# Fetching one column of gathered rows in two of three chunks with plain DMAs from SyncE

## The reference

```python
def _mean_aggregate(x, edge_index, num_nodes):
    src, dst = (edge_index[0], edge_index[1])
    msgs = x[src]
    summed = jax.ops.segment_sum(msgs, dst, num_segments=num_nodes)
    ...
    return summed / jnp.maximum(counts, 1.0)[:, None]
agg = _mean_aggregate(x, edge_index, x.shape[0])
out = agg @ W_l.T + b_l + x @ W_r.T
out = relu(out) + x
```

## Time and profile before

| | us |
|---|---|
| median of three runs | 4668.51 |
| profiled execution, its own time | 4669.47 |
| its span | 4667.1 |
| first gather of layer 1 begins | 2469.35 |
| last gather of layer 1 begins | 4469.16 |
| last store of layer 1's sums issued | 4483.83 |

### The profile page before, as it was taken

One profiled execution on the slowest core, in us unless ns is written; L12 is line 12 of the kernel. 1 busy time (PEld: TensorE's weight loads), 2 busy tenths in 40 slices (PEclk: granted clock), 3 DMA queues, 4 the chain that ended last, 5 costly groups with the idle time before them and its releaser, 6 DMA issues. The chain is left out here.

```text
span 4667.1 us, 26336 instructions
## 1 busy us (share of the span) xinstructions
PE 922.2 (20%) x3111; PEld 611.6 (13%) x3111; DVE 2264.2 (49%) x9482; ACT 397.2 (9%) x994; POOL 3394.4 (73%) x3539
## 2 busy tenths in 40 slices
PE   6301101111120000000292222112222222101036
PEld 6301001011010000000141111001111111100025
DVE  2107665665566656655563434434334334334347
ACT  2001001001010000000051000000000000000015
POOL 6677777777777777777556777777777777777764
PEclk6556555555555555555595555555555555555569
DMA  9813333333333222222285666665666666666669
GB/s 339 307 38 117 119 92 94 119 103 102 100 103 111 77 78 88 87 77 78 89 280 179 209 233 219 210 230 205 215 226 221 218 221 226 218 215 214 208 213 320
DMA packets 347657, 793.59 MB, mean 170 GB/s; under 512 B 78438, under 2 KB 217035, under 8 KB 323972
## 3 DMA queue, kind: packets, MB, share of 16 engines
q1 hardware_dynamic: 150162, 378.14, 23.0%
q0 software_dynamic: 139424, 279.69, 19.8%
q10 hardware_dynamic: 57938, 134.62, 7.6%
HBM read 420.40 MB, written 371.83 MB: 170 GB/s over the span
## 5 line engine op out<-in xcount | busy, mean ns | idle before, releaser
L460 POOL DMA_INDIRECT sb_big<-x,sb_idx x1564 | 1524.3, 975 | 513.1 <-issue 476.5
L460 POOL DMA_INDIRECT sb_big<-zu_rows,sb_idx x1564 | 1479.6, 946 | 490.9 <-issue 476.6
L1264 DVE SCALAR_TENSOR_TENSOR sb_big<-sb_big,sb_keepc 128x256 f32<-128x256 f32 x1518 | 741.8, 489 | 534.6 <-DMA sb_big<-x,sb_idx 481.9
L642 PE MATMUL ps_T<-sb_ident,sb_xg 128*128 128x128 f32 x308 | 87.3, 380 | 2513.7 <-DMA sb_xg<-x 1407.7
L1034 DVE TENSOR_TENSOR sb_big<-ps_V,sb_big 128x2176 f32<-128x2176 f32 x46 | 111.5, 2425 | 596.7 <-DMA sb_big<-zu_rows,sb_idx 596.7
L642 PEld LDWEIGHTS ps_T<-sb_ident,sb_xg 128*128 128x128 f32 x308 | 55.0, 195 | 2558.2 <-issue 1932.0
L1028 DVE TENSOR_TENSOR_SCAN ps_V<-ps_V,sb_big 128x34 f32<-128x34 f32 x2944 | 357.1, 211 | 14.8 <-issue 14.8
L1264 DVE SCALAR_TENSOR_TENSOR sb_big<-sb_scratch,sb_keepc,sb_big 128x256 f32<-128x256 f32 x46 | 22.3, 485 | 697.9 <-DMA sb_big<-x,sb_idx 660.9
L1077 DVE TENSOR_TENSOR_SCAN sb_big<-ps_E,sb_big 128x34 f32<-128x34 f32 x2944 | 355.4, 205 | 1.6
L460 POOL DMA_INDIRECT sb_hn<-rows,sb_nidx x196 | 190.4, 971 | 89.2 <-issue 56.7
L776 ACT COPY sb_tileT<-ps_T 128x256 f32<-128x256 f32 x154 | 56.9, 369 | 1419.1 <-PE ps_T L642 1416.8
(11 more groups left out here) (233 smaller groups left out, 1946.4 us busy)
## 6 DMA issues: line engine op xcount, KB each, us to landing
rows<-sb_big SPq DMA_DIRECT2D x46, 2816.0 KB, 10.1
rows<-sb_big SPq DMA_DIRECT2D x46, 1536.0 KB, 6.0
rows<-sb_big ACTq DMA_DIRECT2D x46, 1224.0 KB, 4.6
z_at_start<-sb_zero ACTq DMA_DIRECT2D x46, 1088.0 KB, 9.5
sb_big<-z_at_start SPq DMA_DIRECT2D x46, 1088.0 KB, 5.0
sb_xg<-in_x_dram SPq DMA_DIRECT2D x42, 768.0 KB, 6.0
own<-sb_hn SPq DMA_DIRECT2D x28, 896.0 KB, 8.9
sb_big<-own SPq DMA_DIRECT2D x28, 896.0 KB, 5.2
```

The source lines that it names most:

```text
L460: pool.indirect_dma_start(to, None, table, bass.IndirectOffsetOnAxis(ap=index.bitcast(U32), axis=0), **more).then_inc(done, 16)
L642: mm = pe.transpose(T[b % depth][:, k * P:(k + 1) * P], xg[0][:, b, k * P:(k + 1) * P], ident[:, :])
L1264: dve.scalar_tensor_tensor(out=slot1[s][:, j, :], in0=before, scalar=keepc[:, j:j + 1], in1=slot1[s][:, j, :], op0=ALU.mult, op1=ALU.add). ...
```

## The change

The last column (33) of a chunk in buffer 0 or 1 is no longer gathered by GpSimd, except in chunk 0. SyncE fetches it: for every partition one plain DMA of one row of 1 KB from `x1` into `slot1[s]`, at a row number that SyncE has in a register. The row numbers come out of `src_i`, first by a DMA of 128 words into a staging row on one partition, then in eight loads of 16 registers. The fetch is in two halves of 64 rows, which stand in SyncE's list behind the first and behind the second store of the chunk two before. VectorE waits for it ahead of column 33 alone. SyncE's last looped round is written out.

```diff
+            rows_at = [sp.alloc_register(f"row{k}") for k in range(RB)]
+            def stage_rows(i, s):
+                    sp.dma_start(stage[0:1, s, :], src_i[:, bass.ds((S1 * i + s) * C + C - 1, 1)]
+                                 ).then_inc(stage_loaded[s], 16)
+            def fetch_rows(i, s, half):
+                if half == 0:
+                    sp.wait_ge(stage_loaded[s], 16 * (i + s))
+                    sp.sem_inc(gate, 1)
+                    wait(sp, r_stored[s], 32 * i)
+                    sp.sem_inc(gate, 1)
+                for p0 in range(half * P // 2, (half + 1) * P // 2, RB):
+                    sp.load(rows_at, stage[0:1, s, p0:p0 + RB])
+                    for k in range(RB):
+                        row = sp.snap(rows_at[k], min_val=0, max_val=N - 1)
+                        sp.dma_start(slot1[s][p0 + k:p0 + k + 1, C - 1, :], x1[bass.ds(row, 1), :]
+                                     ).then_inc(r_fetched[s], 16)
             def store_rows1(i, s):
                 c = S1 * i + s
+                ahead = (i, 2) if s == 0 else (i + 1, s - 1)
+                if by_sync(*ahead):
+                    stage_rows(*ahead)
                 sp.wait_ge(col_summed, c * C + CA)
                 sp.dma_start(edge_cols(rows1, c)[:, 0:CA, :], ...)
+                if by_sync(*ahead):
+                    fetch_rows(*ahead, 0)
                 sp.wait_ge(car1_saved, c + 2)
                 sp.dma_start(edge_cols(rows1, c)[:, CA:C, :], ...)
+                if by_sync(*ahead):
+                    fetch_rows(*ahead, 1)
...
-                for j in range(C):
+                for j in range(C - 1 if by_sync(i, s) else C):
                     gather(slot1[s][:, j, :], x1, idx[s][:, j:j + 1], r_gathered[int(j >= CA)][s])
...
                     elif j == CA:
-                        dve.wait_ge(r_gathered[1][s], 16 * (C - CA) * (i + 1))
+                        rest = C - CA
+                        by_gpsimd = rest + (rest - 1) * i if s == 0 else (rest - (s == 1)) * (i + 1)
+                        dve.wait_ge(r_gathered[1][s], 16 * by_gpsimd)
+                    if j == C - 1 and by_sync(i, s):
+                        dve.wait_ge(r_fetched[s], 16 * P * (i + s))
```

More of the change, by code:

```diff
@@ L75, in gnn_kernel @@
     LOOK = S1 * C
+    RB = 16
     NZ = 4
@@ L191, in gnn_kernel @@
         idx = [sb(f"idx{s}", [P, C], I32) for s in range(S1)]
+        stage = sb("stage", [1, 2, P], I32)
         nidx = [sb(f"nidx{s}", [P, GB], I32) for s in range(2)]
@@ L267, in gnn_kernel @@
         r_stored = sems("r_stored", S1); car1_saved = sem("car1_saved")
+        stage_loaded = sems("stage_loaded", 2); r_fetched = sems("r_fetched", 2)
         DA = 15
@@ L275, in gnn_kernel, with by_sync @@
         block = ctx.enter_context(nc.Block())
+        def by_sync(i, s):
+            first = isinstance(i, int) and i == 0
+            beyond = isinstance(i, int) and S1 * i + s >= NCH
+            return s < 2 and not (first and s == 0) and not beyond
         def edge_cols(dram, c):
@@ L410, in _ @@
                 sp.wait_ge(n_stored[0][s], 32 * (NG // 2))
+            rows_at = [sp.alloc_register(f"row{k}") for k in range(RB)]
+            def stage_rows(i, s):
+                with nc.allow_non_contiguous_dma(reason="a word of each partition"):
+                    sp.dma_start(stage[0:1, s, :], src_i[:, bass.ds((S1 * i + s) * C + C - 1, 1)]
[12 more added lines that the diff above has]
+                                     ).then_inc(r_fetched[s], 16)
             def store_rows1(i, s):
                 c = S1 * i + s
+                ahead = (i, 2) if s == 0 else (i + 1, s - 1)
+                if by_sync(*ahead):
+                    stage_rows(*ahead)
                 sp.wait_ge(col_summed, c * C + CA)
                 sp.dma_start(edge_cols(rows1, c)[:, 0:CA, :], slot1[s][:, 0:CA, :]).then_inc(r_stored[s], 16)
+                if by_sync(*ahead):
+                    fetch_rows(*ahead, 0)
                 sp.wait_ge(car1_saved, c + 2)
                 sp.dma_start(edge_cols(rows1, c)[:, CA:C, :], slot1[s][:, CA:C, :]).then_inc(r_stored[s], 16)
+                if by_sync(*ahead):
+                    fetch_rows(*ahead, 1)
             bg_load(1, 0)
+            stage_rows(0, 1)
+            for half in range(2):
+                fetch_rows(0, 1, half)
             for s in range(S1):
                 store_rows1(0, s)
-            with sp.Fori(1, NG) as i:
+            with sp.Fori(1, NG - 1) as i:
                 bg_store(1, i - 1)
@@ L429, in _ @@
                     store_rows1(i, s)
+            bg_store(1, NG - 2)
+            bg_load(1, NG - 1)
+            for s in range(S1):
+                store_rows1(NG - 1, s)
             bg_store(1, NG - 1)
```

## The result

The changed kernel took 5226.19 us (median of four runs, 5207.68 to 5249.59) against 4660.88 us before on the same chip: a ratio of 1.1202, 95% interval 1.1151 to 1.1253. The 4660.88 us are the median of four runs, the three of before and one more, so the kernel lost 565.3 us. The forecast was 5217 us, 548.5 more than 4668.5. The profiled execution took 5238.41 us, with a span of 5236.3 us.

What follows compares the result with a forecast made beforehand. GpSimd's gathers were taken as the bound before, SyncE after: 3840 fetches at 0.58 us (2227 us) plus 336 us for the rest give a stage of 2563 against 2014.5 us, 548.5 more, so 5217 us; range 4625 to 5750.

Steps and rivals of the forecast that it cites:

- GpSimd's count of gathers is the bound: Layer 1's stage before the change: GpSimd sets the pace at 1.279 us per gather; 30 gathers fewer would remove 38.4 us.
- The signs: Expected in the trace: GpSimd idle about 43 us a round, VectorE waiting at column 33, SyncE's round near 171 us.
- (a): SyncE issuing one fetch DMA of a 1 KB row: 0.25 us taken, bounds 0.25 and 0.35.
- (b): SyncE computing each fetch's address from a register, with the copy by `snap`: 0.27 us taken, bounds 0.20 and 0.27.
- (c): SyncE loading 16 registers from the staging row: 1 us per load taken, 0.06 per fetch, bounds 0.004 to 0.16.
- Together 0.58 us per fetch: SyncE's issue, address and register load summed for one fetch: 0.58 us, bounds 0.45 and 0.78; 3840 fetches take 2227 us.
- (d): Rest of SyncE's round (stores, background and staging DMAs, waits for landings): 22.4 us, 336 us over fifteen rounds.
- First rival: SyncE keeps up if a fetch costs at most 0.45 us; GpSimd then sets the pace, 4630 us; chance 0.21.
- Word by word: Rival: SyncE's register loads go one word at a time, 2.6 us per load, 0.68 per fetch, 5601 us; chance 0.16.
- Held behind stores: Rival: SyncE's fetches stand still behind large stores, 21 us a round, 315 us over 15 rounds, 5532 us; chance 0.13.
- What lies behind the stage isn't touched: Time after layer 1's stage was claimed to stay the same, so nothing was added for it.

## Why the prediction was right

- *GpSimd's count of gathers is the bound, 1.279 us each.* Shown by the kernels where SyncE has room: 30 fewer gave 37.5 us with constant rows and 45 us with two queues, 38.4 forecast.
- *The signs.* GpSimd idles 45.1 us a round, 43 forecast, though the profile names the store `rows<-sb_big` for only a part of it; VectorE waits at column 33; SyncE's round is 171.65 us, 171 forecast.
- *(a) Issue, 0.25 us.* Measured 238 ns, median of 3840.
- *(b) Address, 0.27 us.* Measured 0.438 - 0.238 = 0.20. It was the lower bound: each fetch has one fused register operation (44 ns) and one move (29 ns), as a DMA of before, and the copy of `snap` added no instruction.
- *(c) A load of 16 registers, 1 us.* Median 1.236, and 2.4 to 3.6 for the four of a round that stand behind a store (2.43, 3.05, 3.64 and 2.71, together 11.8). The 16 loads of a round are 26.7 us and not 16. By the Trainium skill ("Runtime: NRT & Kernel Launch", instruction fetch mechanics) it would have been 3.2 us at about 200 ns a register, and by "DMA: Bandwidth & Descriptors" (latency) 0.6; the trace agrees with neither, 1.236 / 16 = 77 ns a register.
- *Together 0.58 us per fetch, 148.5 us a round.* Measured (129.6 + 11.8) / 256 = 0.55, 141.4 us. The address was 18 us a round too high and the loads 11 us too low.
- *(d) The rest, 22.4 us.* Measured 171.65 - 141.4 = 30.2. Its wait was 16.7 us (2896.87 to 2913.6, when the first load began) where 10 was taken; the background DMAs held SyncE 2.8 and not 5.4; the other fetch waited under 1 us (2986.23 to 2987.1) where 2.9 was taken; and the turn of the loop (from the last DMA of its body to the first), not in the sum at all, is 3.06 us (3059.91 to 3062.97), where the earlier trace rows have 0.56 between the last store and L360.

So the sum per round hit 171.65 to within a microsecond since a term 7 us too high met one 8 us too low. The mechanism and its size are shown by the runs without loads and with constant addresses; that the forecast was 9 us off is partly luck, and an error of 0.05 us in one fetch would have been 190 us. Part of the luck is also the base: the kernel before was 4668.5 us in the forecast and 4660.88 in the comparison, so the loss was 565.3 us against 548.5, 17 us more. Between the two profiles it is the other way for the stage, 542.5 against 548.5; the end of the kernel, put at nothing, gave 15.

- *First rival, turning at 0.45 us per fetch.* The runs agree with it. At 0.34 to 0.37, with constant rows, SyncE keeps up. At 0.47, without loads, it doesn't: its round is 149.7 us (2977.60 to 3127.34). The wait for the late store, 17.1 us, is in that; without it the round is 132.6, still over 127.9, and what is left beside the fetches is 13.3, near the 12.4 of this rival. No run stands between 0.37 and 0.47, so the point itself was not measured. The kernel was beyond it by the address and by the hold behind stores, and further by the loads.
- *Word by word.* Wrong: a load takes 1.24 us, not 2.6.
- *Held behind stores.* Present and small: the four loads behind stores take 11.8 us a round instead of 4 x 1.24, which is 7 us where the rival had 21.
- *What lies behind the stage isn't touched.* Wrong by 15 us: the last four stores bunch up, and their landing is waited for.

## What to carry to other kernels

Work handed to an idle queue is priced per instruction and against the time of one round, not against the queue's idle share: 256 fetches of 0.55 us do not fit into 128 us, and everything behind them in the queue's list falls in step. Removing 38 us of work then cost 565. The same work on two queues, each under its round, gave the 1% that was looked for. A wait shown for one DMA tells little of what its removal brings, as long as another wait of nearly the same end stands beside it.

## What the runs showed of the hardware

- A DMA of one 1 KB row holds SyncE 0.24 us, 0.34 with the gap at a constant address in a long run of them (0.37 behind a store), 0.44 at an address from a register (0.46 to 0.50 behind a store, without loads).
- A load of 16 registers from SBUF takes 1.24 us on SyncE and 1.31 on ScalarE, and 2.4 to 3.6 on SyncE where it follows a large store.
- A DMA of 512 bytes issued behind 4.3 MB of stores on the same queue landed after 18.0 us in the round shown (issued at 2895.39), as late as the second of the stores (18.3). Issued at 2985.01, with no store just ahead of it, the same DMA landed after 2.0 us.
- The turn of a loop whose body has grown by 256 fetches of three instructions each took 3.06 us instead of 0.56, and the packets of the instruction queue went from 127 to 250. Without the loads it took 3.0 us (3124.34 to 3127.34). With constant rows, where a fetch is one instruction, it took 0.64 us (3027.66 to 3028.30) and the packets were 135. So it goes with the number of instructions or with the register operations among them, not with the number of DMAs. The Trainium skill ("Runtime: NRT & Kernel Launch", instruction fetch mechanics) says that a taken branch out of the window of fetched pages has to wait for its target; these numbers agree with it, and no run here varied the length of the body alone.
